# Two routers rebuilt in a two-layer graph kernel: norms by tile, eight-largest instructions, a bias as a split row product, stores in two parts

## The reference

```
# layer 0, routed feed-forward: 64 experts share one pair of weights; only the gate depends on the router
logits = x @ router_w.T;  probs, idx = top_k(softmax(logits), 2)
pos = rank of the token within its expert (stable order);  keep = pos < 512
y = gelu(x @ w1.T + b1) @ w2.T + b2
out = sum over the two choices of  y * prob  where keep
# layer 1, routed feed-forward: 8 experts of their own
logits = x @ Wg + bg;  w, idx = top_k(logits, 2);  w = softmax(w)
comb = one_hot(idx) weighted by w                     # tokens x 8
y_e = silu(x @ W1[e] + b1[e]) @ W2[e] + b2[e]
out = sum over e of comb[:, e] * y_e
```

## Time and profile before

| | us |
|---|---|
| three runs, median (lowest to highest) | 914.82 (913.17 to 915.06) |
| profiled execution, its own time | 914.17 |
| its span | 912.4 |
| PE busy | 838.7 (92%) |
| DVE / ACT / POOL busy | 529.6 / 239.3 / 145.0 |
| share of PE in the chain that ended last | 88% |

### The profile page before, as it was taken

How to read it: one execution, slowest core, us unless ns; L and a number is a source line. 1 busy time by engine, 2 the same in 40 slices (tenths; PEclk the granted TensorE clock), 3 DMA queues, 4 the chain that set the end, 5 groups by cost and what they waited for, 6 DMA issues and landing times.

```text
span 912.4 us, 10911 instructions
## 1 busy us (share of the span) xinstructions
PE 838.7 (92%) x4086; PEld 663.7 (73%) x4086; DVE 529.6 (58%) x719; ACT 239.3 (26%) x442; POOL 145.0 (16%) x89
## 2 busy tenths in 40 slices
PE   2999999998999999999968998987689999999993
PEld 1998758856577777754557788867568998898893
DVE  6968999848979999940484153747532112421212
ACT  3142222215411014110244142221353231532210
POOL 2010010030100000020033312500033340442400
PEclk9999999797999997999988998999569999999997
DMA  7733789794687778520212101000052211222001
GB/s 247 211 49 76 231 258 369 259 192 107 162 269 268 231 231 277 166 92 1 89 59 93 47 1 47 1 1 0 1 185 93 93 47 47 92 92 92 0 0 56
DMA packets 64091, 110.21 MB, mean 121 GB/s; under 512 B 6695, under 2 KB 16292, under 8 KB 64052
## 3 DMA queue, kind: packets, MB, share of 16 engines
q1 hardware_dynamic: 54356, 96.71, 31.7%
q0 software_dynamic: 6912, 7.70, 5.5%
q10 hardware_dynamic: 2784, 5.27, 1.6%
HBM read 105.81 MB, written 1.28 MB: 117 GB/s over the span
## 4 chain that ended last, share of the span: by engine, by line
PE 88%; DVE 6%; ACT 2%; issue 1%; DMA 1%; DVEq 0%; SPq 0%; ACTq 0%
PE bank L1193 55%; PE bank L1559 12%; PE bank L1274 6%; PE bank L1397 4%; PE bank L1380 4%; PE bank L1202 2%; PE bank L1391 2%; PE bank L1374 2%; DMA slot<-in_x 1%; DVE st L796 1%; PE bank L1209 1%; ACT slot L547 1%; PE bank L1481 0%; DVE slot L1017 0%; PE bank L1278 0%
## 5 line engine op out<-in xcount | busy, mean ns | idle before, releaser
L948 DVE SCALAR_TENSOR_TENSOR weights<-weights,att 128x2048 f32<-128x2048 f32 x116 | 263.3, 2347 | 3.4 <-DMA weights<-in_L_gnn_basis 2.7
L1193 PE MATMUL bank<-half,ew_hi 128*128 128x312 f32 (+1 forms) x576 | 127.6, 311 | 1.7 <-DVE slot L1167 1.7
L1193 PE MATMUL bank<-AT,slot 125*128 125x312 f32 (+1 forms) x400 | 107.8, 432 | 1.7 <-ACT slot L547 0.9
L1177 DVE CAST hid_hi<-slot 128x626 fp32r<-128x626 f32 x32 | 16.2, 507 | 159.5 <-ACT slot L774 159.5
L1193 PEld LDWEIGHTS bank<-half,ew_hi 128*128 128x128 f32 x576 | 98.7, 192 | 6.4 <-issue 3.6
L1193 PEld LDWEIGHTS bank<-AT,slot 125*128 125x128 f32 x400 | 76.7, 192 | 32.5 <-issue 1.8
L516 POOL TENSOR_TENSOR ew_lo<-weights,ew_hi 128x1024 fp32r<-128x1024 f32 x28 | 69.7, 2509 | 176.4 <-ACT ew_hi L755 176.4
L1193 PE MATMUL bank<-half,ew_lo 128*128 128x312 f32 (+1 forms) x288 | 89.1, 309 | 0.0
L547 ACT ACTIVATE slot<-bank 128x312 f32<-128x312 f32 (+6 forms) x100 | 49.7, 531 | 145.5 <-PE bank L1193 112.4
L1193 PE MATMUL bank<-weights,slot 128*125 128x512 f32 (+5 forms) x306 | 86.1, 450 | 0.0
L1193 PEld LDWEIGHTS bank<-weights,slot 128*125 128x125 f32 (+2 forms) x306 | 53.6, 211 | 28.8 <-issue 25.2
(11 more groups left out here) (258 smaller groups left out, 1073.0 us busy)
## 6 DMA issues: line engine op xcount, KB each, us to landing
weights<-in_L_gnn_basis SPq DMA_DIRECT2D x60, 1024.0 KB, 5.4
weights<-in_L_ffn_W SPq DMA_DIRECT2D x32, 512.0 KB, 4.4
weights<-in_L_mix_kqv_w SPq DMA_DIRECT2D x1, 3072.0 KB, 10.2
weights<-in_w_qkvT SPq DMA_DIRECT2D x3, 1024.0 KB, 5.5
slot<-slot POOLq DMA_DIRECT2D x10, 250.0 KB, 6.1
weights<-in_L_mix_mlp_w ACTq DMA_DIRECT2D x2, 1024.0 KB, 16.5
weights<-in_L_gnn_root ACTq DMA_DIRECT2D x2, 1024.0 KB, 10.0
slot<-in_row_mlp_b POOLq DMA_DIRECT2D x1, 1250.0 KB, 33.6
```

The lines of the kernel that those rows point to most:

```text
L948: ins = dve.scalar_tensor_tensor(wrel[layer][r], wmat(at), att[:, layer, r, b:b + 1], wrel[layer][r], ALU.mult, ALU.add)
L1193: ins = pe.matmul(out, a, b, start=i == 0, stop=i == len(pairs) - 1)
```

## The change

It does the following.
- Both norms ahead of `xn2` and `xe` go tile by tile (`layernorm_by_tile`), with the transposes of a tile as soon as its row is there. The router logits of tile j-1 follow the transposes of tile j. In the first router the adjacency blocks move from behind `hf` to between those transposes (`xn2A`, 12 PSUM tiles).
- `top_two` is gone. `largest` takes the eight largest of each tile's row (MAX), `one_hots` their positions (MAX_INDEX) and compares them with an index row. The softmax is no longer normalised over the table: only the sum and the gap of the two largest are used.
- `chosen`, the triangle and the ones are half precision (`tri16`, `ones16`); the cut at 512 and the multiplication are one instruction.
- `ffn_b2` comes in by PE: a 33-row product of ones with `b2_split` (rounded part and remainder on partitions 0 and 32), in the same group as `fy`; DVE reads `fy` from PSUM. ACT's copies and POOL's adds go.
- In the second router ACT writes columns and `xe_hi` per tile and POOL subtracts `xe_lo` per tile. `comb` and the bias are split likewise (72 rows: high at 0 to 7, low at 32 to 39, high again at 64 to 71), so that `eb2` is a product of rounded operands.
- The expert list is signalled before its length; the loop starts without waiting for the bias adds, since its banks are now planned (`eh`).
- PE signals each output tile at the last step (`y_last`), and a store is two transfers, of 112 and of 13 rows.

```diff
-            sqrt_by_tile("xf_row", 0)
-            transposed("xfT", col(2))
+            for j in range(TT + 1):
+                if j < TT:
+                    sqrt_of_tile("xf_row", 0, j)
+                if j:
+                    columns_of("xfT", j - 1, j - 1, col(2))
...
+            for j in range(TT + 1):
+                if j < TT:
+                    sqrt_of_tile("xe_row", 0, j)
+                if j:
+                    tile = B("xeT", j - 1)[:, 0:KT * P].rearrange("p (k t) -> p k t", k=KT)
+                    act.wait_ge(S("psum_full"), filled("xeT", j))
+                    act.activation(col(2)[:, :, P * j - P:P * j], tile, ACT.Copy).then_inc(S("xe_col"), 1)
+                    copy_out("xeT", j - 1, xe_hi[:, :, P * j - P:P * j], tile)
             act.wait_ge(S("el_sub"), 1)
             act.activation(eexp, eexp, ACT.Exp).then_inc(S("el_exp"), 1)
+            link(act.activation(small[0:1, 1010:1011], eps[0:1, 0:1], ACT.Silu))
...
+            def largest(val):
+                for j in range(TT):
+                    ins = dve.max(mx8[:, j, :], val[:, j, :])
+                link(ins)
+            def one_hots(val, e, hot, idx):
+                for j in range(TT):
+                    ins = dve.max_index(ix8[:, j, :], mx8[:, j, :], val[:, j, :])
+                link(ins)
+                link(dve.tensor_copy(idx, ix8[:, :, 0:2]))
+                for i in range(2):
+                    ins = dve.tensor_tensor(hot[i], iota_bc(e), idx[:, :, i:i + 1].to_broadcast([P, TT, e]), ALU.is_equal)
+                link(ins)
...
+            def x2_row(j):
+                dve.wait_ge(S("psum_full"), filled("fy", j + 1))
+                dve.scalar_tensor_tensor(x[:, j, :], B("fy", j)[0:P, :], gate[:, j:j + 1], x[:, j, :],
+                                         ALU.mult, ALU.add).then_inc(S("fy_out"), 1)
+                dve.wait_ge(S("fy_out"), j + 1)
+            layernorm_by_tile(x, row(1), "xn2_row", x2_row)
...
+            for j in range(TT):
+                tile_to_cols("xn2A", XN2_TILE[j], j, row(1), "xn2_row")
+                if j < TT - 1:
+                    adjacency_T(j)
+            for n in range(4, 7):
+                adjacency_T(n)
...
-            top_two(U[0], E1, [U[1], U[2], U[3], U[4]], [b1, b2], 1e30)
-            link(dve.tensor_tensor(U[4], U[2], U[3], ALU.add))
+            largest(U[0])
+            link(dve.tensor_tensor(U[1], U[0], mx8[:, :, 1:2].to_broadcast([P, TT, E1]), ALU.is_ge))
...
+            for j in range(TT):
+                pool.wait_ge(S("xe_col"), j + 1)
+                pool.wait_ge(S("act_read"), READ0["xeT"] + j + 1)
+                pool.tensor_tensor(xe_lo[:, :, P * j:P * j + P], col(2)[:, :, P * j:P * j + P],
+                                   xe_hi[:, :, P * j:P * j + P].bitcast(f32), ALU.subtract).then_inc(S("xe_low"), 1)
...
-                group(bk[0:P, :], [(combT[:, P * j:P * j + P], eb2)]).then_inc(S("psum_full"), 1)
-            pe.wait_ge(S("eb2_out"), 5)
-            pe.wait_ge(S("elist"), 1)
-            pe.wait_ge(S("xe_low"), 1)
+                group(bk[0:P, :], [(combT[:, P * j:P * j + P], eb2_split)]).then_inc(S("psum_full"), 1)
...
+                    if j < TT - 1:
+                        dve.wait_ge(S("y_last"), (TT - 1) * it + j + 1)
+                    else:
+                        dve.wait_ge(S("y_mm"), 16 * it + 16 + Y0)
...
-                sp.dma_start(out[P * j:P * j + P, :], x[:, j, :]).then_inc(S("stored"), 16)
+                for a, n in ROW_PARTS:
+                    sp.dma_start(out[P * j + a:P * j + a + n, :], x[a:a + n, j, :]).then_inc(S("stored"), 16)
```

More of the change, by code:

```diff
@@ L72 @@
 ROW_PARTS = ((0, 112), (112, 13))
+XN2_TILE, ANT_TILE = (0, 2, 4, 6, 8), (1, 3, 5, 7, 9, 10, 11)
 def basis_sem(at):
@@ L284, in gps_two_layers @@
         iota_e = sb("iota_e", [128, E0])
+        chosen = slot[6][0:P, 1920:1920 + TT * E0 // 2].bitcast(f16).rearrange("p (j e) -> p j e", j=TT)
+        comb72 = half[6][0:P, 1, 0:72 * TT].rearrange("p (j e) -> p j e", j=TT)
         def B(stage, n=0):
@@ L1121, in _, with x3_row @@
                                          ALU.add, ALU.add).then_inc(S("xp_out"), 1)
-            for j in range(TT):
+            rev = small[0:1, 800:808]
+            dve.tensor_scalar(rev, iota_e[0:1, 0:E1], -1.0, float(E1), ALU.mult, ALU.add)
+            def x3_row(j):
                 dve.wait_ge(S("psum_full"), filled("x3r", j + 1))
                 dve.tensor_tensor(x[:, j, :], B("x3r", j)[0:P, :], x[:, j, :], ALU.add).then_inc(S("x3r_out"), 1)
-            layernorm(x, row(1), "xe_row", wait="x3r_out")
-            dve.wait_ge(S("xe_high"), 1)
-            dve.tensor_tensor(xe_lo[:, :, 0:N], col(2)[:, :, 0:N], xe_hi[:, :, 0:N].bitcast(f32), ALU.subtract).then_inc(S("xe_low"), 1)
+                dve.wait_ge(S("x3r_out"), j + 1)
+            layernorm_by_tile(x, row(1), "xe_row", x3_row)
             U = [table(6, i, E1) for i in range(6)]
@@ L1156, in _ @@
+            dve.wait_ge(S("elist"), 1)
+            link(dve.tensor_scalar(srt, srt, 0.5, None, ALU.is_ge))
+            link(dve.tensor_reduce(key1[:, 0:1], srt, AX.X, ALU.add))
             dve.tensor_copy(el_i[0:1, 8:9], key1[:, 0:1]).then_inc(S("elist"), 1)
+            one_hots(U[0], E1, U[2:4], idx)
             dve.wait_ge(S("el_exp"), 1)
@@ L1413, in _ @@
                 ins.then_inc(S("psum_full"), 1)
[L1414 removed]
+            pe.wait_ge(S("A_mean"), 5)
             for j in range(TT):
[L1416 to L1428 removed]
+                tile_to_cols("xn2A", XN2_TILE[j], j, row(1), "xn2_row")
+                if j < TT - 1:
+                    adjacency_T(j)
+            for n in range(4, 7):
+                adjacency_T(n)
+            pe.wait_ge(S("act_read"), READ0["xn2A"] + XN2_TILE[1] + 1)
             pe.wait_ge(S("Wqkvo_in"), 64)
@@ L1527, in _, with expert_logits @@
             to_rows("x3r", col(6))
-            to_cols("xeT", row(1), "xe_row")
+            def expert_logits(j):
+                pe.wait_ge(S("xe_col"), j + 1)
+                return group(B("el")[0:P, E1 * j:E1 * j + E1], [(col(2)[:, k, P * j:P * j + P], Wg[:, k, :]) for k in range(KT)])
             pe.wait_ge(S("Wg_in"), 32)
-            small_rows("el", col(2), Wg, E1, columns="xeT")
+            for j in range(TT):
+                tile_to_cols("xeT", j, j, row(1), "xe_row")
+                if j == 1:
+                    claim(pe, "el")
+                if j:
+                    expert_logits(j - 1)
+            expert_logits(TT - 1).then_inc(S("psum_full"), 1)
             bk = claim(pe, "en")
```

208 lines of the change are left out of this document (117 added, 91 removed), and 12 rows, old and new, of tables (ACT_READS, PSUM_ORDER).

## The result

| us | before | after |
|---|---|---|
| median of four runs each, same chip | 914.0 (913.16 to 915.06) | 888.2 (886.45 to 892.5) |
| profiled execution, its span | 914.17, 912.4 | 887.52, 885.8 |

The ratio is 0.9731 (95% interval 0.9697 to 0.9765), or 25.8 us less. 888.8 had been forecast, within 882 to 896.

The account below looks back on a forecast made before the run. TensorE (PE) was taken to set the pace nearly everywhere, other engines counting only where it waits. Terms 0 - 7.6 - 8.9 - 9.3 = -25.8 from 914.17 gave 888.4, with part of the median's 0.65 888.8; range 882 to 896.

Parts of the forecast that it names:

- First norm: First router's input norm and logits: no change, 0 us, bounds -1.0 and +1.
- First selection and gate: First router, logits to gate: shorter selection and half-precision counts bring the gate at 465.15 instead of 473.96, -8.8 us.
- Slower: Both routers' selections: MAX and MAX_INDEX cost far more than other reads, from 1.4 us each eating the whole 25.8; chance 0.01.
- x2 rows and norm by tile: First router, second norm: the tile chain costs DVE +1.2 us; -7.6 taken for this router, bounds -5 and -9.
- Second norm and logits: Second router: PE binds at half clock, logits at 651.4 instead of 653.97, -2.6 us.
- Second selection to the loop: Second router, logits to expert loop: 12.7 us instead of 19.05, the weight split being late next, -6.35 us.
- Loop: Expert loop: all PE (239 us) and stays, its first 5 us at half clock.
- Tail: After PE's last product: early adds and stores in parts end 4.4 us behind PE instead of 13.7, -9.3 us.
- The clock: Second router rival: PE holds 2.4 GHz, DVE binds, the loop starts without slow time, -6.5 us, 882; chance 0.12.
- The stores: Tail rival: stores stay slow at 125 GB/s, the end 11.5 us behind PE, 896; chance 0.08.
- The lock: Second router rival: POOL's `xe_lo` subtractions hold DVE's norm, logits at 653.6, +2.2 us, 891; chance 0.07.

Follow-up runs that it names:

- roots_ahead: Changed kernel with ScalarE's square roots moved ahead of column copies in the first norm; PE's first transpose to first logits' copy 7.16 us instead of 8.17.
- index_doubled: Changed kernel with each router's five MAX_INDEX done twice; first logits' copy to gate +1.11 us, second logits to expert loop +0.80.
- both_orders_new: Changed kernel with square roots ahead of column copies (first norm) and transposed expert weights copied by VectorE; median 885.1 us, ratio to before 0.9688.
- norm_two_batch: Changed kernel with the second router's norm back to one square root for all five tiles; first x3 add to second logits 21.12 us, +3.74.
- comb_copy_vector: Changed kernel with the two copies of the transposed expert weights on VectorE instead of ScalarE; second logits to expert loop 10.92 us instead of 12.69.
- stores_two_queues: Changed kernel with 112-row stores issued by SyncE and 13-row ones by ScalarE; 5.01 us from PE's last product to the end.

## Why the prediction was right, point by point

- **First norm, 0.** T to L1 8.17 against 8.24. Both halves are shown: the hold costs 1.0, and without it (roots_ahead, 7.16) the interleaved logits are 1.1 faster than before.
- **First selection and gate, -8.8.** L1 to G -9.06. The pair at 0.20 lay at the assumed place; index_doubled shows that it is all path. The half-precision counts took 1.03 us, not 1.7. "Slower" would have needed 1.4 us an instruction. The term compared the new sum with the old times as they stood, and so held the 2.0 us of the old selection beside POOL without naming them.
- **x2 rows and norm by tile, +1.2.** To the last row it is +1.4 (11.26 against 9.82 behind G), and from L1 to the last row -7.6, as taken. The prediction put all 4.40 us of transposes behind that row, where 2.7 stood. So G to Q is +0.67 or +2.3, by where the clock falls. In the profile of the changed kernel it does not fall at all in this stretch (1.00 in every window from 440 to 488), and the 1.65 us come back as a loss by X: G to X is 161.4 to 162.3 in ten profiles with this code, whichever way it went (160.6 in both_orders_new), and 159.6 and 160.5 in the two with the old code. From L1 to X the kernel of before took 176.5, the changed one 169.3: -7.1, where **-7.6** had been taken. Read at Q alone, the gain would be 8.4 in this profile and 6.7 in those where the clock fell.
- **Second norm and logits, -2.6.** -3.08. PE was the limit at half clock, as forecast; norm_two_batch shows the term.
- **Second selection to the loop, -6.35.** -6.36. The number was right, and the reason only half. I had costed the first split as late by the load and ScalarE's work; what holds it is that ScalarE copies the weights' transpose and then enters the loop, 1.8 us behind the landing (index_doubled, comb_copy_vector).
- **Loop, 0.** -0.8: 0.34 up to the second expert's first product, where the clock comes back sooner at the start, and 0.47 at the change of experts and behind it, where early adds take DVE out of PE's way. That second part was missing from the sum. (The 239 us named for the loop hold the tail; by the markers it is 225.7.)
- **Tail, -9.3.** -8.5. The mechanism was right and the size a little off. The term's own parts (begun 1 us ahead of PE's end, 3.2 to 4.3 of transfer, 2.4 of latency) add up to 4.6 to 5.7 behind PE, not to 4.4; the measured 5.25 lies within. Two parts missed against each other: the stores began 1.87 ahead, and ran at 248 to 269 GB/s where 300 to 400 was assumed.
- **Rivals.** The clock stayed at 0.50 in the second router. The stores were not slow. The lock struck once there, a normalising tensor_scalar of 1.26 us instead of 0.55 beside `xe_lo`, off the path since PE was late anyway. Where late adds make it cost 7 us, at the change of experts, I had not looked for it.

The sum by markers, from L1 on: -7.1 - 3.1 - 6.4 - 0.8 - 8.5 = -25.9, against -25.8 forecast (T to L1 and what lies ahead make up the other 0.7 of 26.6). That the total is met so closely is luck: the terms missed by 0.5, 0.5, 0, 0.8 and 0.8, and the misses cancel, while single runs of the changed kernel lie between 886.45 and 892.5. What the runs bear out is the terms, each within 1 us.

## What to carry to other kernels

Cut a path into markers and compare those, not whole times: steps that the clock does not touch repeat to 0.02 us here, where runs of one kernel differ by 5. A saving on an engine shows only up to the next one in line, so double or move one small piece to find which. And look at the row count of a transfer: 125 rows instead of 112 and 13 cost 5.5 us here, more than the five adds ahead of the stores (3.4).

## What the runs showed of the hardware that I had not expected

- Here a cast or a subtraction of VectorE that started behind a subtraction of GpSimd waited for its end: 0.49 became 2.66 us, 0.81 became 2.83. A shift of adds by 3 us turned a near miss into 7.1 us.
- A 33-row piece of 512 columns costs 0.43 us of PE's time beside a full-precision product of 128 rows that takes 1.05, while five of 72 rows take 2.50 at half clock.
- What a kept clock gave was taken back. The seven profiles that reached Q 1.65 us sooner (13.21 instead of 14.86) needed 1.5 to 2.6 us more from Q to X (0.6 to 0.9 in both_orders_new). The windows between Q and X show where it went. Added up, the clock is at half for 6.8 us in the three profiles that had lost it before Q (Q to X 146.5 to 146.8) and in both_orders_new (147.4), for 10.3 in three others (148.3 to 148.4) and for 13.7 in the remaining four (148.8 to 149.1). The same place some 123 us behind Q, in the changed kernel and in stores_two_queues:

```profile
600.00:604.00 4.00, 3.70 (x25) 3.51 (x24) 0.26 (x1) 0.00 (x0) 0.00 (x0) 0.77 0.02 4
...
605.00:609.00 4.00, 3.05 (x21) 2.56 (x20) 1.01 (x3) 0.43 (x2) 0.00 (x0) 1.00 0.02 4
```

  Why the clock falls at another place then is open; no run held the clock by itself.
